# First half of a conv-attention block: the diagonal taps move around the wait for normalised tokens, and VectorE's taps are interleaved anew

## The chip, the cores and the metric

One core of a Trainium2 chip runs the whole program. The metric is the device time of one execution in microseconds (us); the value of a kernel is the median of its runs. The engines are TensorE (PE in the profile; PEld is its weight load), VectorE (DVE), ScalarE (ACT), GpSimd (POOL) and the DMA queues, most of them issued by SyncE (SP).

## What is computed

The input is an image of 192 channels by 128 x 128 positions. The first half is a channel attention with a 3 x 3 depthwise convolution, the second a mixture of experts over all positions:

```python
xn  = layernorm over channels (x)                       # per position, twice nested
qkv = einsum('bchw,oc->bohw', xn, w_qkv)                # 192 -> 576 channels
qkv = depthwise 3x3 convolution (qkv, w_dw)             # 9 taps per channel
q, k, v = split(qkv) * spatial_interaction
attn = softmax(normalised(q) @ normalised(k)^T * temperature)   # 8 heads, 24 x 24 each
x = x + w_proj @ (attn @ v)
x = x + top-2 of 4 experts (192 -> 768 -> 192, gelu)
```

The change lies in the first half, in the part that makes q and k: normalise, project, nine taps of the depthwise convolution, multiply by `spatial_interaction`, and sum up the products of q and k.

## The kernel before

The first half runs over 32 blocks of four image rows (512 positions). Every engine has its own instruction stream, a function `step(i)` written out by hand and called for i = -2 to 34; the middle of it is a hardware loop over pairs of steps. The engines meet only in semaphores. One call of `step(i)` works on several blocks at once: i + 2 is loaded and its moments are taken, i + 1 is normalised, i is transposed and projected, n = i - 1 goes through the convolution, m = i - 2 is turned and goes into the sum of products.

In a step, block by block:

- VectorE normalises four rows into `tn` (L625, "tn" below). ScalarE completes the tile (L538, `tn_dup`), TensorE transposes it in eight pieces (L744), ScalarE copies the result rounded to `xh_a` and `x_c` (L491, L493), and VectorE writes the remainders `xl_a` and `x_c` (L596, L598, semaphore `lo_ok`).
- TensorE projects, `z(i, 0..4)` (L735), five passes each, and ScalarE evicts each to `zwin` (L468) or `zv` (L474). The PSUM banks for z are two, so z(i, ct) waits for the eviction of z(i, ct - 2).
- The nine taps of the three channel tiles (ct = 0, 1, 2) are shared out. TensorE does three, two and two of them with diagonal matrices: `dw(n, ct)` (L693), two passes per tap. VectorE adds five, six and six more: `tap(n, ct, k)` (L589), in which k = 0 reads TensorE's PSUM bank and the others read and write `acc` in SBUF. ScalarE makes the ninth (L484), GpSimd adds it (L411) and multiplies by `spatial_interaction` (L414).
- ScalarE takes squares of the result (L508), TensorE turns it four rows in sequence, `q_tr(m, t)` (L709), ScalarE copies it (L459), and `gram(m, t)` (L721) sums up the products.
- For block i + 2, TensorE transposes x (L764, L765), which needs the banks that `lo_ok` sets free, ScalarE copies it to `xtok` (L525), VectorE takes moments (bn_stats L618, aggregate L634), and GpSimd makes the inverse deviation of them in seven small operations (L428 to L435).

The engine's order in a step is what the change edits. TensorE: transposes of tn, dw 0, dw 1, q_tr 0, x transposes, q_tr 1, gram 0, z 0, q_tr 2, gram 1, z 1, q_tr 3, gram 2, dw 2, gram 3, z 2, z 3, z 4. VectorE: xl_a, x_c, taps 0.0, 0.1, 0.2, 1.0, 0.3, 1.1, 0.4, 1.2, 1.3, 1.4, 1.5, 2.0, then bn_stats and taps 2.1 to 2.4 in turn with tn before tap 2.4, the aggregates, tap 2.5 (c.k is channel tile and number of the tap). Successive taps of one tile each wait for the tap before. ScalarE and GpSimd keep their order.

In two early and four late steps ScalarE and GpSimd also split expert weights into two parts (L546, L447), whose stores the next such split waits for.

Of the kernel before, what the change touches and what calls it, by code (L numbers as in the profile page):

```python
# [19 lines left out]
ALU = mybir.AluOpType  # L20
# [25 lines left out]
PE_TAPS = [[0, 1, 2], [0, 1], [0, 1]]  # L46
DVE_TAPS = [[3, 4, 5, 6, 7], [2, 3, 4, 5, 6, 7], [2, 3, 4, 5, 6, 7]]
POOL_TAP = 8
HEAD_START = 2
CX = C + E  # L50
CY = CX + E
C3 = 3 * C + E
# [66 lines left out]
def build(nc, x, spat, ln_w, ln_b, w_qkv, w_dw, w_proj, temperature, gate_w, gate_b, w1, b1, w2, b2, out):  # L119
    top = ExitStack()  # L120
    with top:
# [45 lines left out]
        with p1:  # L167
# [401 lines left out]
            def _(dve):  # L569
                def window_ready(n):  # L570
                    if n.within(0, NB - 1):
                        dve.wait_ge(z_a, 5 * n.val + QK)
                    wait(dve, carry, n.val)
                    if n.static and n.val == NB:
                        dve.wait_ge(row_z, 1)
# [15 lines left out]
                        scalar=wdw[:, ct, DVE_TAPS[ct][k]:DVE_TAPS[ct][k] + 1], in1=before, op0=ALU.mult, op1=ALU.add).then_inc(dw_l[ct], 1)  # L591

                def step(i):
                    if i.within(0, NB - 1):
                        dve.wait_ge(hi_ok, 2 * i.val + 1)
                        nc.vector.tensor_tensor(xl_a[:, 0, :], tp[0][:, :], xh_a[:, 0, :].bitcast(FP32), ALU.subtract).then_inc(lo_ok, 1)  # L596
                        dve.wait_ge(hi_ok, 2 * i.val + 2)
                        nc.vector.tensor_tensor(x_c[CB:128, 0, :], tp[1][CB:128, :], x_c[CB:128, 0, :].bitcast(FP32), ALU.subtract)\  # L598
                            .then_inc(lo_ok, 1)
                    n = i - 1  # L600

                    if n.within(0, NB):
                        window_ready(n)
                        for k in range(HEAD_START):
                            tap(n, 0, k)
                        for k in range(n_dve[1]):
                            if k + HEAD_START < n_dve[0]:
                                tap(n, 0, k + HEAD_START)
                            tap(n, 1, k)
                    b, a = i + 2, i + 1  # L610
                    if n.within(0, NB):
                        tap(n, 2, 0)
                    if b.within(0, NB - 1):
                        dve.wait_ge(xt_a, 2 * b.val + 2)
                        wait(dve, r_ok, 2 * b.val - 2)
                    for t in range(ROWS):
                        if b.within(0, NB - 1):
                            last = nc.vector.bn_stats(stat[:, b.par, t, :], xtok[:, b.par, t, 0:C])  # L618
                            if t == ROWS - 1:
                                last.then_inc(bn_ok, 1)  # L620
                        if t == ROWS - 1 and a.within(0, NB - 1):
                            wait(dve, ac_t, 2 * a.val)
                            dve.wait_ge(r_ok, 2 * a.val + 2)
                            for u in range(ROWS):
                                last = nc.vector.tensor_scalar(tn[:, u, 0:C], xtok[:, a.par, u, 0:C], mv[:, a.par, u, 0:1],  # L625
                                                               rs_all[:, bass.ds(a.val * ROWS + u, 1)], ALU.subtract, ALU.mult)
                            last.then_inc(tn_ok, 1)
                        if n.within(0, NB):
                            tap(n, 2, t + 1)
                    if b.within(0, NB - 1):  # L630
                        dve.wait_ge(bn_ok, b.val + 1)
                        nc.vector.memset(pause[:, 0:1], 0.0)
                        for t in range(ROWS):
                            last = nc.vector.bn_aggr(mv[:, b.par, t, :], stat[:, b.par, t, :])  # L634
                        last.then_inc(stats, 1)
                    if n.within(0, NB):
                        for k in range(ROWS + 1, n_dve[2]):
                            tap(n, 2, k)

                def setup():  # L640

# [34 lines left out]
            def _(pe):  # L676
# [59 lines left out]
                    last.then_inc(z_t, 1)  # L736

                def step(i):
                    if i.within(0, NB - 1):
                        pe.wait_ge(tn_dup, i.val + 1)  # L740
                        wait(pe, xt_a, 2 * min(i.val + 2, NB) if i.static else 2 * i.val + 4)
                        for h in (0, 1):
                            for t in range(ROWS):
                                last = nc.tensor.transpose(tp[h][:, t * 128:t * 128 + 128], tn[:, t, h * 128:h * 128 + 128], ident[:, :])  # L744
                            last.then_inc(ac_t, 1)
                    n, m = i - 1, i - 2
                    has_i, has_n, has_m = i.within(0, NB - 1), n.within(0, NB), m.within(0, NB)
                    if has_n:
                        dw(n, 0)
                        dw(n, 1)  # L750
                    if has_m:
                        q_tr(m, 0)
# [14 lines left out]
                    if has_m:  # L767
                        q_tr(m, 1)
                        gram(m, 0)
                    if has_i:  # L770
                        z(i, 0)
                    if has_m:
# [4 lines left out]
                    if has_m:  # L777
                        q_tr(m, 3)
                        gram(m, 2)
                    if has_n:  # L780
                        dw(n, 2)
                    if has_m:
                        gram(m, 3)
                    if has_i:
                        z(i, 2)
# [1087 lines left out]
```

## Time and profile before

| | us |
|---|---|
| median of 3 runs | 2479.31 |
| lowest and highest | 2478.91, 2484.78 |
| the profiled execution | 2480.38 |
| its span in the profile | 2478.6 |
| TensorE busy | 2095.3 (85%) |
| VectorE busy | 1535.2 (62%) |
| ScalarE busy | 1233.2 (50%) |
| GpSimd busy | 1059.1 (43%) |
| mean granted TensorE clock | 0.934 of full |

All times in the profile count from the start of the span. The first half ends at about 725 us. A record of the profile has a start, a duration and an engine; "x4" on a line means that four records in a row are merged into one. Records of one engine can overlap by under 0.1 us, so what an instruction costs in a stream is the distance from start to start. Since the steps repeat, one whole step, here from the tn at 427.40 to the next, can be read in place of all.

### The profile page before, as it was taken

What the parts mean: (1) busy time and instruction counts of PE and PEld (TensorE: products, weight loads), DVE (VectorE), ACT (ScalarE), POOL (GpSimd) and SP (SyncE); (2) the same over time, 40 slices, a digit from 0 to 9 for tenths busy, and PEclk for the clock granted to TensorE, in tenths of its full rate; (3) what the DMA queues carried; (4) which work ended last, traced back from release to release, by engine and by line L of the source; (5) the groups of instructions that cost most, each with busy time, mean ns of one, the idle gap of its engine ahead of it and who ended that gap; (6) DMA issues with size and microseconds to landing.
All of it is one profiled execution on the core that took longest, in us unless ns stands there. A gap on an engine that the chain in (4) does not pass through costs nothing.

```text
span 2478.6 us, 37518 instructions
## 1 busy us (share of the span) xinstructions
PE 2095.3 (85%) x10924; PEld 1693.3 (68%) x10924; DVE 1535.2 (62%) x3350; ACT 1233.2 (50%) x2152; POOL 1059.1 (43%) x1154
## 2 busy tenths in 40 slices
PE   6788888888766786139999999999999999999992
PEld 3455555555543455129988889888888998898991
DVE  5688988898782334516766646675544666565652
ACT  3455555556443441014554545555555565566661
POOL 3556555665664321640065410277400036742424
PEclk9899999999887997559999999999999999999995
DMA  4242222222314566446676666669655658776753
GB/s 121 73 122 70 70 70 70 73 71 73 90 57 109 155 161 183 150 167 203 210 249 204 239 201 200 201 231 319 214 168 179 195 188 297 246 254 204 247 186 108
DMA packets 297499, 410.82 MB, mean 166 GB/s; under 512 B 27642, under 2 KB 228602, under 8 KB 297340
## 3 DMA queue, kind: packets, MB, share of 16 engines
q1 hardware_dynamic: 272764, 350.13, 44.9%
q0 software_dynamic: 24576, 58.75, 7.3%
q8 instruction: 77, 1.26, 0.2%
q14 instruction: 82, 0.67, 0.1%
HBM read 265.73 MB, written 143.07 MB: 165 GB/s over the span
## 4 chain that ended last, share of the span: by engine, by line
PE 43%; POOL 10%; issue 4%; DMA 2%; DVE 2%; ACT 0%; SPq 0%; POOLq 0%; ACTq 0%; DVEq 0%
PE bank L1749 18%; PE bank L1767 11%; POOL xs_scratch L1336 7%; PE bank L1768 5%; POOL yg L1349 4%; PE bank L1800 4%; PE bank L1792 3%; PE bank L1773 2%; DMA xs_scratch<-xn,idx 1%; DMA yg<-y_scratch,ydx 0%; PE bank L1818 0%; PE bank L1821 0%; DVE fin L1677 0%; DVE x L1448 0%; DVE hl L1719 0%
## 5 line engine op out<-in xcount | busy, mean ns | idle before, releaser
L1767 PE MATMUL bank<-w_hl,hh 128*128 x1824 | 552.7, 356 | 25.5 <-DVE hl L1719 21.9
L1719 DVE TENSOR_TENSOR hl<-hf,hh 128x512 fp32r<-128x512 f32 x456 | 314.3, 690 | 385.0 <-ACT hh L1390 384.2
L1387 ACT ACTIVATE hf<-bank,b_col 128x512 f32<-128x512 f32 x456 | 314.3, 689 | 465.7 <-PE bank L1749 465.5
L1768 PE MATMUL bank<-w_hl,hl 128*128 x1824 | 460.4, 252 | 0.0
L589 DVE SCALAR_TENSOR_TENSOR acc<-zwin,wdw,acc 128x512 f32<-128x512 f32 (+2 forms) x462 | 423.6, 935 | 6.5
L1767 PEld LDWEIGHTS bank<-w_hl,hh 128*128 128x128 f32 x1824 | 345.4, 189 | 51.6 <-issue 30.4
L1768 PEld LDWEIGHTS bank<-w_hl,hl 128*128 128x128 f32 x1824 | 350.3, 192 | 21.2
L1349 POOL DMA_INDIRECT yg<-y_scratch,ydx x256 | 257.9, 1007 | 223.2 <-DMA y_scratch<-yo 77.3
L1336 POOL DMA_INDIRECT xs_scratch<-xn,idx x256 | 258.4, 1010 | 131.5 <-issue 75.9
L1749 PE MATMUL bank<-p2xh_a,w1b 128*128 128x512 f32 x912 | 308.3, 419 | 4.2 <-DVE p2x_c L1713 2.1
L1390 ACT ACTIVATE hh<-hf 128x512 fp32r<-128x512 f32 x456 | 287.9, 631 | 14.5
L1749 PE MATMUL bank<-p2x_c,w1b 128*128 128x512 f32 x912 | 289.8, 399 | 0.0
L1356 POOL TENSOR_TENSOR rstd<-mv,pw 128x4 f32<-128x4 f32 x32 | 7.0, 220 | 602.8 <-DVE mv L1462 602.7
L411 POOL TENSOR_TENSOR last_tap<-acc,last_tap 128x512 f32<-128x512 f32 (+2 forms) x99 | 135.2, 1365 | 250.6 <-DVE acc L589 248.5
L693 PE MATMUL bank<-zwin,diag 128*128 128x512 f32 (+2 forms) x462 | 213.2, 603 | 8.5 <-issue 8.5
L1749 PEld LDWEIGHTS bank<-p2x_c,w1b 128*128 128x128 f32 x912 | 173.3, 190 | 41.2
L1749 PE MATMUL bank<-p2xl_a,w1b 128*128 128x512 f32 x456 | 182.5, 400 | 0.0
L1663 DVE TENSOR_REDUCE yo<-bank 128x192 f32<-128x384 f32 x304 | 148.3, 551 | 34.3 <-PE bank L1768 34.1
L693 PEld LDWEIGHTS bank<-zwin,diag 128*128 128x128 f32 x462 | 87.2, 203 | 89.0 <-issue 87.5
L414 POOL TENSOR_TENSOR qs<-last_tap,s_bc 128x512 f32<-128x512 f32 (+2 forms) x99 | 144.0, 1455 | 7.8
L1749 PEld LDWEIGHTS bank<-p2xh_a,w1b 128*128 128x128 f32 x912 | 140.1, 192 | 6.2 <-ACT hf L1387 3.3
L1792 PE MATMUL bank<-ident,xs 128*128 128x128 f32 x608 | 85.7, 285 | 64.1 <-DMA xs<-xs_scratch 64.1
(252 smaller groups left out, 3484.4 us busy)
## 6 DMA issues: line engine op xcount, KB each, us to landing
w1b<-w1s_scratch SPq DMA_DIRECT2D x152, 768.0 KB, 4.7
xs<-xs_scratch SPq DMA_DIRECT2D x76, 512.0 KB, 5.5
y_scratch<-yo SPq DMA_DIRECT2D x76, 384.0 KB
zr<-v_scratch SPq DMA_DIRECT2D x64, 240.0 KB, 3.3
xtok_scratch<-xtok SPq DMA_DIRECT2D x32, 384.0 KB, 2.6
v_scratch<-zv SPq DMA_DIRECT2D x64, 192.0 KB
vc_scratch<-cv SPq DMA_DIRECT2D x64, 192.0 KB, 2.5
vd<-vc_scratch SPq DMA_DIRECT2D x64, 192.0 KB
```

The source lines that it names most:

```text
L589: nc.vector.scalar_tensor_tensor(out=a, in0=zwin[n.par][:, ct, ky + lo:ky + hi, kx:kx + W], scalar=wdw[:, ct, DVE_TAPS[ct][k]:DVE_TAPS[ct] ...
L693: last = nc.tensor.matmul(db[(n.par + ct) % 2][:, lo * W:hi * W].rearrange("p (r w) -> p r w", w=W), diag[:, ct, k, :], zwin[n.par][:, ct, ...
L1336: nc.gpsimd.indirect_dma_start(xs_dram, bass.IndirectOffsetOnAxis(ap=idx[:, h, b * NT + t:b * NT + t + 1], axis=0), src, None).then_inc(st ...
L1349: nc.gpsimd.indirect_dma_start(yg[:, s % 2, h, t, :], None, y_dram[g], bass.IndirectOffsetOnAxis(ap=ydx[:, h, s * ROWS + t:s * ROWS + t + ...
L1387: nc.scalar.activation(hf[:, k % 3, :], lb[k % 2][:, :], ACT.Gelu, bias=b1_col[:, bass.ds(exp_of[J] * CH + k, 1)]).then_inc(gelu, 1)
L1390: nc.scalar.activation(hh[:, k % 3, :], hf[:, k % 3, :], ACT.Copy).then_inc(hh_ok, 1)
L1663: nc.vector.tensor_reduce(out=yo[:, J % 2, t, :], in_=yb[t][:, 0:2 * C].rearrange("p (h c) -> p c h", h=2), axis=AX, op=ALU.add).then_inc( ...
L1719: nc.vector.tensor_tensor(hl[:, k % 3, :], hf[:, k % 3, :], hh[:, k % 3, :].bitcast(FP32), ALU.subtract).then_inc(hl_ok, 1)
L1749: last = nc.tensor.matmul(lb[k % 2][:, :], w[:, q, :], v[:, J % 2, :], start=(i == 0), stop=(i == 4))
L1767: nc.tensor.matmul(yb[t][:, 0:2 * C], hh[:, k % 3, cols], w, start=(k == 0), stop=False, skip_group_check=True)
L1768: last = nc.tensor.matmul(yb[t][:, 0:C], hl[:, k % 3, cols], w[:, 0:C], start=False, stop=(k == CH - 1), skip_group_check=True)
L1792: last = nc.tensor.transpose(mb[h][:, t * 128:t * 128 + 128], xs[:, J % 2, t, h * 128:h * 128 + 128], ident[:, :])
```

## The change

TensorE: `dw(n, 0)` is issued ahead of the wait for `tn_dup` and the transposes of tn. `dw(n, 2)` moves from behind gram 2 to the place between gram 0 and z 0. VectorE: the three first taps of tile 0 (`HEAD_START` 3 in place of 2) are issued ahead of the waits for `hi_ok` and of xl_a and x_c. Then tile 1's taps alternate with the last two of tile 0 and, from tap 1.2 on, with 2.0 to 2.2. The four bn_stats stand together, followed by tap 2.3, tn, tap 2.4, the aggregates and tap 2.5. No instruction is added or removed.

```diff
--- before.py
+++ after.py
@@ -46,7 +46,7 @@
 PE_TAPS = [[0, 1, 2], [0, 1], [0, 1]]
 DVE_TAPS = [[3, 4, 5, 6, 7], [2, 3, 4, 5, 6, 7], [2, 3, 4, 5, 6, 7]]
 POOL_TAP = 8
-HEAD_START = 2
+HEAD_START = 3
 CX = C + E
 CY = CX + E
 C3 = 3 * C + E
@@ -591,51 +591,51 @@
                         scalar=wdw[:, ct, DVE_TAPS[ct][k]:DVE_TAPS[ct][k] + 1], in1=before, op0=ALU.mult, op1=ALU.add).then_inc(dw_l[ct], 1)
 
                 def step(i):
+                    n, a, b = i - 1, i + 1, i + 2
+                    has_n = n.within(0, NB)
+                    if has_n:
+                        window_ready(n)
+                        for k in range(HEAD_START):
+                            tap(n, 0, k)
                     if i.within(0, NB - 1):
                         dve.wait_ge(hi_ok, 2 * i.val + 1)
                         nc.vector.tensor_tensor(xl_a[:, 0, :], tp[0][:, :], xh_a[:, 0, :].bitcast(FP32), ALU.subtract).then_inc(lo_ok, 1)
                         dve.wait_ge(hi_ok, 2 * i.val + 2)
                         nc.vector.tensor_tensor(x_c[CB:128, 0, :], tp[1][CB:128, :], x_c[CB:128, 0, :].bitcast(FP32), ALU.subtract)\
                             .then_inc(lo_ok, 1)
-                    n = i - 1
-
-                    if n.within(0, NB):
-                        window_ready(n)
-                        for k in range(HEAD_START):
-                            tap(n, 0, k)
-                        for k in range(n_dve[1]):
-                            if k + HEAD_START < n_dve[0]:
-                                tap(n, 0, k + HEAD_START)
+                    if has_n:
+                        for k in range(n_dve[0] - HEAD_START):
                             tap(n, 1, k)
-                    b, a = i + 2, i + 1
-                    if n.within(0, NB):
-                        tap(n, 2, 0)
+                            tap(n, 0, k + HEAD_START)
+                        for k in range(n_dve[0] - HEAD_START, n_dve[1]):
+                            tap(n, 1, k)
+                            if k + 1 < n_dve[1]:
+                                tap(n, 2, k - (n_dve[0] - HEAD_START))
                     if b.within(0, NB - 1):
                         dve.wait_ge(xt_a, 2 * b.val + 2)
                         wait(dve, r_ok, 2 * b.val - 2)
-                    for t in range(ROWS):
-                        if b.within(0, NB - 1):
+                        for t in range(ROWS):
                             last = nc.vector.bn_stats(stat[:, b.par, t, :], xtok[:, b.par, t, 0:C])
-                            if t == ROWS - 1:
-                                last.then_inc(bn_ok, 1)
-                        if t == ROWS - 1 and a.within(0, NB - 1):
-                            wait(dve, ac_t, 2 * a.val)
-                            dve.wait_ge(r_ok, 2 * a.val + 2)
-                            for u in range(ROWS):
-                                last = nc.vector.tensor_scalar(tn[:, u, 0:C], xtok[:, a.par, u, 0:C], mv[:, a.par, u, 0:1],
-                                                               rs_all[:, bass.ds(a.val * ROWS + u, 1)], ALU.subtract, ALU.mult)
-                            last.then_inc(tn_ok, 1)
-                        if n.within(0, NB):
-                            tap(n, 2, t + 1)
+                        last.then_inc(bn_ok, 1)
+                    if has_n:
+                        tap(n, 2, 3)
+                    if a.within(0, NB - 1):
+                        wait(dve, ac_t, 2 * a.val)
+                        dve.wait_ge(r_ok, 2 * a.val + 2)
+                        for t in range(ROWS):
+                            last = nc.vector.tensor_scalar(tn[:, t, 0:C], xtok[:, a.par, t, 0:C], mv[:, a.par, t, 0:1],
+                                                           rs_all[:, bass.ds(a.val * ROWS + t, 1)], ALU.subtract, ALU.mult)
+                        last.then_inc(tn_ok, 1)
+                    if has_n:
+                        tap(n, 2, 4)
                     if b.within(0, NB - 1):
                         dve.wait_ge(bn_ok, b.val + 1)
                         nc.vector.memset(pause[:, 0:1], 0.0)
                         for t in range(ROWS):
                             last = nc.vector.bn_aggr(mv[:, b.par, t, :], stat[:, b.par, t, :])
                         last.then_inc(stats, 1)
-                    if n.within(0, NB):
-                        for k in range(ROWS + 1, n_dve[2]):
-                            tap(n, 2, k)
+                    if has_n:
+                        tap(n, 2, 5)
 
                 def setup():
 
@@ -736,17 +736,18 @@
                     last.then_inc(z_t, 1)
 
                 def step(i):
-                    if i.within(0, NB - 1):
+                    n, m = i - 1, i - 2
+                    has_i, has_n, has_m = i.within(0, NB - 1), n.within(0, NB), m.within(0, NB)
+                    if has_n:
+                        dw(n, 0)
+                    if has_i:
                         pe.wait_ge(tn_dup, i.val + 1)
                         wait(pe, xt_a, 2 * min(i.val + 2, NB) if i.static else 2 * i.val + 4)
                         for h in (0, 1):
                             for t in range(ROWS):
                                 last = nc.tensor.transpose(tp[h][:, t * 128:t * 128 + 128], tn[:, t, h * 128:h * 128 + 128], ident[:, :])
                             last.then_inc(ac_t, 1)
-                    n, m = i - 1, i - 2
-                    has_i, has_n, has_m = i.within(0, NB - 1), n.within(0, NB), m.within(0, NB)
                     if has_n:
-                        dw(n, 0)
                         dw(n, 1)
                     if has_m:
                         q_tr(m, 0)
@@ -767,6 +768,8 @@
                     if has_m:
                         q_tr(m, 1)
                         gram(m, 0)
+                    if has_n:
+                        dw(n, 2)
                     if has_i:
                         z(i, 0)
                     if has_m:
@@ -777,9 +780,6 @@
                     if has_m:
                         q_tr(m, 3)
                         gram(m, 2)
-                    if has_n:
-                        dw(n, 2)
-                    if has_m:
                         gram(m, 3)
                     if has_i:
                         z(i, 2)
```

## Rows read from the trace of the kernel before

**Rows 1.** Busy time by stage: the steps from 137.9 to 611.4 (columns in the first line)
```profile
core 0: us, PE busy (x) PEld busy (x) DVE busy (x) ACT busy (x) POOL busy (x), PEclk, DMA share, GB/s
137.90:611.40 473.50, 413.21 (x1909) 271.42 (x1909) 424.65 (x738) 273.87 (x552) 282.54 (x299) 0.97 0.25 73
```
**Rows 2.** Timeline of VectorE, one step: start, us, engine, line, operation, count, idle before
```profile
427.40 1.23 DVE L625 TENSOR_SCALAR tn<-xtok,mv,rs_all 128x192 f32<-128x192 f32 x4
...
429.52 0.71 DVE L589 SCALAR_TENSOR_TENSOR acc<-zwin,wdw,acc 128x512 f32<-128x512 f32 x1
430.62 0.69 DVE L596 TENSOR_TENSOR xl_a<-bank,xh_a 128x512 fp32r<-128x512 f32 x1 [0.39 <-ACT xh_a L491]
...
432.92 0.75 DVE L589 SCALAR_TENSOR_TENSOR acc<-zwin,wdw,bank 128x512 f32<-128x512 f32 x1 [0.89 <-PE bank L693]
...
447.55 1.23 DVE L625 TENSOR_SCALAR tn<-xtok,mv,rs_all 128x192 f32<-128x192 f32 x4
```
**Rows 3.** Busy time by stage: the step before that one
```profile
405.90:427.40 21.50, 18.86 (x83) 12.55 (x83) 18.49 (x33) 11.99 (x24) 12.16 (x13) 0.92 0.24 67
```
**Rows 4.** Busy time by stage: two stretches around the start of that step
```profile
403.70:407.10 3.40, 1.43 (x7) 0.70 (x5) 3.40 (x9) 0.69 (x1) 0.55 (x1) 1.00 0.00 0
407.10:410.50 3.40, 2.77 (x10) 2.26 (x11) 2.48 (x10) 2.37 (x5) 1.51 (x2) 0.50 0.00 0
```
**Rows 5.** Timeline of TensorE, the step of rows 2
```profile
429.22 1.09 PE L744 MATMUL bank<-ident,tn 128*128 128x128 f32 x8 [2.64 <-ACT tn L538]
430.14 4.46 PE L693 MATMUL bank<-zwin,diag 128*128 128x512 f32 x10
...
434.76 0.27 PE L764 MATMUL bank<-ident,xc_a 128*128 128x128 f32 x1
...
437.22 0.48 PE L735 MATMUL bank<-xh_a,wq_ah 128*128 128x512 f32 x1
...
440.32 0.49 PE L709 MATMUL bank<-ident,qs 128*128 128x128 f32 x3
...
440.98 1.91 PE L693 MATMUL bank<-zwin,diag 128*128 128x512 f32 x4
...
446.34 0.40 PE L735 MATMUL bank<-x_c,wq_cl 128*100 128x512 f32 x1
```
**Rows 6.** Who waited for whom, 137.9 to 611.4: total us, times, longest
```profile
PE bank L744 <- ACT tn L538: 60.3, 23, 2.7
```
**Rows 7.** Timeline of ScalarE, the same step
```profile
428.66 0.42 ACT L538 ACTIVATE tn<-tn 128x256 f32<-128x256 f32 x1 [2.43 <-DVE tn L625]
...
441.85 0.68 ACT L468 ACTIVATE zwin<-bank,bz 128x512 f32<-128x512 f32 x1
```
**Rows 8.** Timeline of VectorE, single taps of the same step
```profile
433.70 0.75 DVE L589 SCALAR_TENSOR_TENSOR acc<-zwin,wdw,acc 128x512 f32<-128x512 f32 x1
434.49 0.75 DVE L589 SCALAR_TENSOR_TENSOR acc<-zwin,wdw,acc 128x512 f32<-128x512 f32 x1
...
436.48 0.75 DVE L589 SCALAR_TENSOR_TENSOR acc<-zwin,wdw,acc 128x512 f32<-128x512 f32 x1
437.14 0.75 DVE L589 SCALAR_TENSOR_TENSOR acc<-zwin,wdw,acc 128x512 f32<-128x512 f32 x1
...
438.59 1.66 DVE L589 SCALAR_TENSOR_TENSOR acc<-zwin,wdw,acc 128x512 f32<-128x512 f32 x1
```
**Rows 9.** Timeline of GpSimd, the same step: third pair, first pair's addition
```profile
430.38 1.29 POOL L411 TENSOR_TENSOR last_tap<-acc,last_tap 128x512 f32<-128x512 f32 x1 [4.65 <-DVE acc L589]
431.75 1.28 POOL L414 TENSOR_TENSOR qs<-last_tap,s_bc 128x512 f32<-128x512 f32 x1
...
438.06 1.63 POOL L411 TENSOR_TENSOR last_tap<-acc,last_tap 128x512 f32<-128x512 f32 x1 [0.78 <-DVE acc L589]
```
**Rows 10.** Timeline of GpSimd and VectorE, a late step: the first of four tn
```profile
632.50 1.59 POOL L414 TENSOR_TENSOR qs<-last_tap,s_bc 128x512 f32<-128x512 f32 x1
633.17 1.05 DVE L625 TENSOR_SCALAR tn<-xtok,mv,rs_all 128x192 f32<-128x192 f32 x1
```
**Rows 11.** Timeline of ScalarE, an early step with expert weights
```profile
96.42 0.52 ACT L546 ACTIVATE wph<-stage 128x384 fp32r<-128x384 f32 x1 [9.18 <-DMA w1s_scratch<-wpl]
```

## The prediction, made before the changed kernel ran

> Tap c.k below is the k-th tap that VectorE adds for channel tile c, `tap(n, c, k)`; dw0 to dw2 are TensorE's diagonal taps `dw(n, 0..2)`; "tn" is the normalising step of L625. All times are us.
>
> **What bounds the kernel now.** I first split the span by stage. The lines of the change run from about 30 to 725; the 23 steps between 137.9 and 611.4 take 473.5 us, 20.6 each, and in them VectorE is busy 90% and TensorE 87% [rows 1]. So neither is free, and the order decides. Two whole steps show the period: 20.15 at full clock (tn at 427.40 and again at 447.55 [rows 2]), and 21.5 for the one before [rows 3]. In the longer one the granted clock is at the lower of its two levels, 1.2 GHz, for 3.4 us, just after TensorE had sat idle 2.6 [rows 4, 5]. Steps of this second kind make up what 23 x 20.15 = 463.5 leaves over: 10.0 us in all. The waits name one gap per step on TensorE: 60.3 us in 23 waits for ScalarE's copy of tn, which itself waits for VectorE's tn [rows 6]. This is the wait that the change fills. The loop through it closes like this: tn 1.23, ScalarE's copy and the start of TensorE 0.59 (428.63 to 429.22), eight transposes 0.92, dw0 at 0.43 a pass for six passes 2.58, a start of 0.2, then tap 0.0 at 432.92 and 14.63 of VectorE without a real gap up to the next tn [rows 2, 5, 7]. The sum is 20.15.
>
> Those 14.63 are not all work. A tap takes 0.75, and the next starts 0.66 after it if it adds to another tile (436.48 to 437.14), 0.79 after it if it adds to the same one (433.70 to 434.49) [rows 8]. While GpSimd runs one of its two 1.28 us additions or products, a tap with both inputs in SBUF takes 1.66 instead, and ends 0.55 after GpSimd's operation; GpSimd, caught in turn behind a tap, takes 1.63 [rows 8, 9]. A tn under GpSimd took 1.05 in place of 0.37, ending 0.12 after it [rows 10]; it happened once, so it is a weak row. xl_a, with one input in PSUM, took 0.69 beside GpSimd [rows 2, 9]. So three pairs of GpSimd operations per step are three places where VectorE can lose up to 0.9 twice. Today the third pair falls on xl_a, x_c and VectorE's idle time and costs nothing.
>
> **The change part by part.** TensorE: dw0 goes ahead of the wait for tn. It is 2.58 of work against 2.64 of idle time [rows 5, 6], so alone it would take away the wait. Nothing needed by dw0 is late: its window was evicted before. What queues behind it is the eight transposes, from 1.8 to about 3.9 after the start of tn, then ScalarE's two copies of them; xl_a no longer cares, since it now stands behind tap 0.2. dw2 ahead of z(i,0) costs something: between q_tr(m,3) and z(i,2) there used to be 1.75 of dw2 that covered ScalarE. Without it z(i,2) could begin 0.94 after q_tr(m,3), but the eviction of z(i,0) ends at 442.53, 2.2 after 440.32, and TensorE starts 0.14 after such a copy (429.08 to 429.22) [rows 5, 7]: 1.4 of TensorE idle comes back there. No DMA issue is moved; the x transposes come about 1.1 later after tn, and the loads and stores that wait for them have most of a step to spare: zero, and a few tenths if that cover went.
>
> VectorE: the instructions are the same, 17 taps, 2 splits, 4 bn_stats, 4 tn, 4 aggregates. Pairs on the same tile fall from five to two, worth 3 x 0.13 = 0.4. But taps 0.0 to 0.2 now stand where the third GpSimd pair runs, and tn where the second runs. I lay the new step out from the start of tn at 0, by the durations above:
> - tap 2.5 starts at 2.1 as today (429.52), and GpSimd's third pair runs from 3.0 to 5.65 [rows 2, 9].
> - Tap 0.0 reads PSUM and isn't held. It starts when dw0 is done, at 4.1 (below). Tap 0.1 is held to 6.2, 0.2 ends at 7.0, xl_a at 7.6, x_c at 8.35.
> - Taps 1.0, 0.3, 1.1, 0.4 run freely and end at 11.1. GpSimd's first pair starts at 11.3, is caught behind tap 1.2 (12.9), and its second half ends at 14.3. Tap 2.0 reads PSUM and starts at 12.9, with dw2's end (below). Tap 1.3 ends 0.55 after GpSimd, at 14.85.
> - Taps 2.1, 1.4, 2.2, 1.5 at 0.66: the bn_stats start at 17.4 and, with as many columns as a tn, at most at its pace of 0.29 [rows 2]; tap 2.3 is due at 18.5.
> - GpSimd's second pair starts at 17.65. It holds tap 2.3 to 19.5, is held by it, and ends at 20.65. The first tn ends at 20.75 instead of a nominal 19.75, and the last at 21.6. Since that was at 1.23 in this step, the period is **20.37**.
>
> TensorE's loop within this: the x transposes start at 8.5 (x_c plus 0.15). From their start to z(i,0) it takes 2.46 today (to 437.22), dw2 adds 1.75, with 0.2 that is the 12.9. Today they reach the end of the last z pass in 11.8 (434.76 to 446.34 and 0.23 for the pass) [rows 5]; with the 1.4 above 13.2, dw0 2.58 and 0.2 make 24.5, which is 4.1 of the next step. Tap 0.0 could be 1.3 later before it passed the hold on tap 0.1, so TensorE no longer sets the step; the hand-over between VectorE and GpSimd does. TensorE is still idle for about 3 a step, in pieces of 1.7 (before the x transposes), 0.5 and 0.9.
>
> The Trainium skill's page "SBUF — State Buffer", section "Who interferes with whom", speaks against this change: whichever of a GpSimd operation and a VectorE operation with two SBUF inputs starts first has the shared ports for its whole length, the other blocks fully, and tensor_scalar can be caught as well. By the rows a held tap ends 0.55 after GpSimd [rows 8, 9], by the page it would need its whole 0.75 after it: an estimate from that page is 0.2 more for each of four holds, 0.8 a step.
>
> **Clock.** Bounds: no low stretch (0), or as many as now (10.0 in 23 steps). The longest idle piece shrinks, the total stays; I take a third, 3.3. The page "TensorE: Matmul & The Clock Gate", section "A second HAM failure mode: psum-queue depth-cycling", says that frequent short pauses make the clock swing too, by which all of the 10.0 would stay; no row here decides it.
>
> **Sum.** Steady stretch: 23 x 20.37 + 3.3 = 471.8 against 473.5, -1.7. In two steps ScalarE hangs on stores of expert weights (one wait 9.2 [rows 11]); there VectorE can do three taps ahead of xl_a (2.2), but dw2 at the lower clock then limits tap 2.0: I take 0.8 of each, bounds 0 and 2.2, so -1.6. In the last two steps, with four same-tile pairs fewer, -0.5. Together -3.8 on an execution of 2480.38 (span 2478.6), 1.07 above the median: 2479.31 - 3.8 = **2475.5**.
>
> **The rivals.**
> - *Holds are cheaper* (0.20): tn isn't held (rows 10 show it once), or GpSimd gets in at other moments. The hand-over loses up to 1.0, and TensorE's own loop is next: 3.65 from tap 0.0 to x_c with nothing held, 0.15, 13.2, 2.58, 0.2, so 19.8. With 0.14 for the clock that is 0.65 below today's 20.59: -15.0 in 23 steps, -2.1 outside them, 2462, and 2456 to 2471 for parts of it.
> - *The filled wait counts in full* (0.03): 2.64 x 31 steps, 2398. Against it stands that VectorE is 90% busy already.
> - *One more tap is held* (0.20): if GpSimd's third pair starts later than tap 0.0, because ScalarE's last tap or the small chain delays it, both 0.1 and 0.2 are held in front of x_c, 0.9 more. It decides as soon as 0.2 is held at all, as this loop has no slack. All of it makes 21.4 a step with the clock, 18.7 more in 23 steps, less the 2.1: 2496. Half makes 2486; middle 2491.
> - *It doesn't do what it says* (0.07): TensorE still waits for tn after dw0, because tn slides with it. Steps as now, 2479.
> - The forecast itself has 0.50, with its own range of 2470 to 2485.
>
> Faster or slower by 0.3% is 7.4 us, about what a measurement of this kernel tells from no change: below 2471.9 lie the first two rivals and a tail of the forecast, 0.26; above 2486.7 the third and a tail, 0.22; between 0.52. The range is 2462 to 2491: it takes in most of the cheaper holds and half of the added one.
>
> **What the profile will show.** TensorE's wait for ScalarE's tn should fall from 60.3 to near zero, with new waits on VectorE's x_c (1.7) and on ScalarE's eviction before z(i,2) (0.9). VectorE should idle about 1.2 before tap 0.0 and 1.1 before 2.0; tap 0.1, 1.3, 2.3 and the first tn should be long ones, tap 0.2 short. If all four tn take 0.37, or the period is under 20, the held tn was the wrong step; if tap 0.2 is long as well, the order of the third pair was.

## The result, and the profile after

The changed kernel takes 2497.74 us (median of 4 runs, 2494.59 to 2498.43) against 2479.57 for the kernel before: a ratio of 1.0066, 95% interval 1.0049 to 1.0084. It is slower, and above the forecast range of 2462 to 2491.

The profiled execution is the shortest of the four, 2494.59 us with a span of 2492.8, 14.2 above the span before. By stage, with the borders put at the same places of the work:

| stage | before | after | difference |
|---|---|---|---|
| up to the 6th tn | 137.9 | 134.5 | -3.4 |
| 23 steps, 6th to 29th tn | 473.5 | 488.6 | +15.1 |
| from there to the last tap | 130.1 | 128.5 | -1.6 |
| the rest, unchanged code | 1737.1 | 1741.2 | +4.1 |

The busy time of two single steps, of the 23 steps and of the rest (columns as in [rows 1]):

```profile
core 0: us, PE busy (x) PEld busy (x) DVE busy (x) ACT busy (x) POOL busy (x), PEclk, DMA share, GB/s
432.00:452.30 20.30, 18.44 (x87) 12.06 (x86) 17.39 (x33) 11.88 (x25) 12.60 (x14) 1.00 0.23 71
345.90:368.40 22.50, 20.11 (x81) 12.69 (x80) 17.42 (x33) 11.76 (x24) 12.57 (x14) 0.85 0.22 64
134.50:623.10 488.60, 441.03 (x1909) 285.62 (x1908) 398.92 (x737) 272.37 (x552) 289.35 (x300) 0.94 0.24 71
751.60:2492.80 1741.20, 1498.87 (x8234) 1302.13 (x8234) 917.37 (x2269) 834.72 (x1340) 631.38 (x689) 0.92 0.63 202
```

There are two kinds of steps here as before [rows 2, 3], but the mix is another. A step at full clock takes 20.34 (20.15 before). The others take 21.3 to 22.8, the granted clock is down in each of them (0.85 or 0.92 over the step), and they are 13 of the 23, where there were 7 before: the mean is 21.24 a step, 20.59 before. Of the +15.1, 23 x 0.19 = 4.4 is the longer full-clock step; the low clock takes 488.6 - 23 x 20.34 = 20.8 where it took 10.0 before, +10.8.

VectorE in a step at full clock, tn at the end (timeline, columns as in [rows 2]; the lines are L589 taps, L602/L604 the splits, L618 bn_stats, L626 tn):

```profile
457.15 0.75 DVE L589 SCALAR_TENSOR_TENSOR acc<-zwin,wdw,bank 128x512 f32<-128x512 f32 x1 [1.07 <-PE bank L693]
457.93 2.27 DVE L589 SCALAR_TENSOR_TENSOR acc<-zwin,wdw,acc 128x512 f32<-128x512 f32 x2
460.12 0.68 DVE L602 TENSOR_TENSOR xl_a<-bank,xh_a 128x512 fp32r<-128x512 f32 x1
460.83 0.69 DVE L604 TENSOR_TENSOR x_c<-bank,x_c 64x512 fp32r<-64x512 f32 x1
...
466.10 0.75 DVE L589 SCALAR_TENSOR_TENSOR acc<-zwin,wdw,bank 128x512 f32<-128x512 f32 x1 [1.14 <-PE bank L693]
466.76 3.90 DVE L589 SCALAR_TENSOR_TENSOR acc<-zwin,wdw,acc 128x512 f32<-128x512 f32 x5
470.58 1.12 DVE L618 BATCH_NORM_STATS2 stat<-xtok 128x6 f32<-128x192 f32 x4
471.63 1.03 DVE L589 SCALAR_TENSOR_TENSOR acc<-zwin,wdw,acc 128x512 f32<-128x512 f32 x1
472.59 2.21 DVE L626 TENSOR_SCALAR tn<-xtok,mv,rs_all 128x192 f32<-128x192 f32 x4
```

and GpSimd beside it:

```profile
456.24 1.28 POOL L411 TENSOR_TENSOR last_tap<-acc,last_tap 128x512 f32<-128x512 f32 x1 [2.75 <-DVE acc L589]
457.59 1.27 POOL L414 TENSOR_TENSOR qs<-last_tap,s_bc 128x512 f32<-128x512 f32 x1
```

Taps 0.1 and 0.2 together take 2.27 instead of 1.54: the first is held until 459.41, 0.55 after GpSimd's 458.86. The four tn take 2.21 instead of 1.23. So the holds stand where the layout put them. VectorE waits 1.07 before tap 0.0 and 1.14 before tap 2.0 (forecast 1.2 and 1.1). In seven of the ten steps at full clock the wait before tap 0.0 is longer, 1.59 to 1.66, and taps 0.1 and 0.2 take only 1.70 to 1.77: tap 0.0 starts about 0.5 later, tap 0.1 ends with GpSimd all the same, and the step keeps its 20.34. So it is the hand-over between VectorE and GpSimd that sets the full-clock step, and not TensorE's dw0, as the layout said.

Who waited for whom in the 23 steps (total, times, longest), to set beside [rows 6]:

```profile
DVE acc L589 <- PE bank L693: 86.6, 46, 4.1
PE bank L765 <- DVE x_c L604: 26.3, 22, 1.6
PE bank L735 <- ACT zwin L468: 14.0, 23, 0.6
```

The wait for tn is gone, and the two new waits that were forecast stand in its place, both shorter than forecast: up to 1.6 for x_c (1.7), 0.61 before z(i,2) (0.9). VectorE's waits for TensorE's diagonal taps were 32.1 in all and 2.6 at the longest before. A place where the clock falls, TensorE's timeline and then the two stretches around it (columns as in [rows 4]):

```profile
417.89 0.49 PE L709 MATMUL bank<-ident,qs 128*128 128x128 f32 x3
419.88 0.33 PE L765 MATMUL bank<-ident,xc_a 128*128 128x128 f32 x1 [1.50 <-DVE x_c L604]
420.14 0.27 PE L766 MATMUL bank<-ident,xc_b 64*128 64x64 f32 x1
420.34 0.33 PE L765 MATMUL bank<-ident,xc_a 128*128 128x128 f32 x1
420.60 0.27 PE L766 MATMUL bank<-ident,xc_b 64*128 64x64 f32 x1
```

```profile
417.80:421.20 3.40, 1.90 (x10) 1.06 (x8) 3.34 (x6) 3.04 (x9) 3.03 (x5) 1.00 0.61 186
421.20:424.60 3.40, 3.40 (x12) 2.42 (x12) 2.06 (x4) 1.66 (x5) 2.37 (x4) 0.51 0.39 114
```

TensorE waits 1.50 for x_c, then makes the x transposes, small products at a distance of 0.2 to 0.26, and after that its clock is at the lower level for 3.4 us, just when dw2 is due. Tap 2.0 waits for dw2, and with it VectorE: the longest such wait has grown from 2.6 to 4.1.

### The profile page after: what moved, and what is told of

The parts are those of the page before. It is cut to its first block, busy times and chain, and to the rows that moved or that the text cites. A ratio compares the mean times of both kernels' runs of the same rounds, so it can differ in the third digit from the quotient of the medians.

```text
span 2492.8 us, 37518 instructions
## 1 busy us (share of the span) xinstructions
PE 2124.7 (85%) x10924; PEld 1707.6 (69%) x10924; DVE 1503.1 (60%) x3350; ACT 1231.4 (49%) x2152; POOL 1070.4 (43%) x1154
## 3 DMA queue, kind: packets, MB, share of 16 engines
q8 instruction: 77, 1.26, 0.2%
## 4 chain that ended last, share of the span: by engine, by line
PE 43%; POOL 9%; issue 4%; DMA 2%; DVE 2%; ACT 1%; SPq 0%; POOLq 0%; ACTq 0%; DVEq 0%
PE bank L1749 18%; PE bank L1767 11%; POOL xs_scratch L1336 6%; PE bank L1768 5%; PE bank L1800 4%; POOL yg L1349 3%; PE bank L1792 3%; PE bank L1773 2%; DMA xs_scratch<-xn,idx 1%; DMA yg<-y_scratch,ydx 1%; PE bank L1818 0%; PE bank L1821 0%; DVE x L1448 0%; DVE fin L1677 0%; DVE hl L1719 0%
## 5 line engine op out<-in xcount | busy, mean ns | idle before, releaser
L589 DVE SCALAR_TENSOR_TENSOR acc<-zwin,wdw,acc 128x512 f32<-128x512 f32 (+2 forms) x462 | 363.0, 826 | 2.6
L693 PE MATMUL bank<-zwin,diag 128*128 128x512 f32 (+2 forms) x462 | 231.1, 633 | 10.7 <-issue 10.7
L589 DVE SCALAR_TENSOR_TENSOR acc<-zwin,wdw,bank 128x512 f32<-128x512 f32 (+2 forms) x99 | 72.3, 731 | 118.4 <-PE bank L693 117.4
L414 POOL TENSOR_TENSOR qs<-last_tap,s_bc 128x512 f32<-128x512 f32 (+2 forms) x99 | 136.5, 1379 | 7.8
```

The costliest lines, as they stand in the source:

```text
L414: nc.gpsimd.tensor_tensor(qs[:, n.par, ct, lo:hi, :], last_tap[:, ct, lo:hi, :], s_bc[:, n.par, lo:hi, :], ALU.mult).then_inc(qs_ok, 1)
L589: nc.vector.scalar_tensor_tensor(out=a, in0=zwin[n.par][:, ct, ky + lo:ky + hi, kx:kx + W], scalar=wdw[:, ct, DVE_TAPS[ct][k]:DVE_TAPS[ct] ...
L693: last = nc.tensor.matmul(db[(n.par + ct) % 2][:, lo * W:hi * W].rearrange("p (r w) -> p r w", w=W), diag[:, ct, k, :], zwin[n.par][:, ct, ...
```

## The experiments

The second half, whose code no kernel here changes, took from 1736 to 1965 us depending on the chip, so ratios are always to the kernel before on the same chip. What decides is the mean of the 23 steady steps from the profile. It repeats: the changed kernel has 21.24 twice, and e10 and e15, one kernel on two chips, have 19.33 both. A "low stretch" is a stretch of some us in which the granted clock is at the lower of its two levels. "Extra matmuls" multiply the identity with itself into a part of a PSUM bank that nobody reads: they keep TensorE busy and do no work of the kernel.

```python
def fill(k):
    for _ in range(k):
        nc.tensor.matmul(gb[0:G2, 256:384], ident[:, 0:G2], ident[:, :], start=False, stop=False, skip_group_check=True)
```

| kernel | mean steady step | granted clock in them | ratio to before |
|---|---|---|---|
| before | 20.59 | 0.97 | |
| changed | 21.24 | 0.94 | 1.0066 |
| changed, again | 21.24 | 0.94 | 1.0056 |
| e1 TensorE's order alone | 20.27 | 0.96 | 0.9963 |
| e2 VectorE's order alone | 28.44 | 0.82 | 1.0802 |
| e3 changed, 12 extra before the x transposes | 21.19 | 1.00 | 1.0040 |
| e5 changed, 6 extra there | 20.33 | 1.00 | 0.9982 |
| e6 changed, extra before gram 3 and z2 | 21.20 | 0.94 | 1.0047 |
| e4 before, 20 extra before tn's transposes | 21.67 | 1.00 | 1.0119 |
| e8 before, 10 extra there | 20.15 | 1.00 | 0.9960 |
| e12 before, dw0 moved | 20.41 | 0.92 | 0.9994 |
| e13 the same, 4 extra | 19.70 | 1.00 | 0.9909 |
| e9 TensorE's order, extra in three places | 19.62 | 1.00 | 0.9919 |
| e10 changed, xl_a and x_c first, extra as e6 | 19.33 | 1.00 | 0.9917 |
| e14 changed, xl_a and x_c first, no extra | 19.33 | 1.00 | 0.9888 |
| e15 as e10 | 19.33 | 1.00 | 0.9865 |

**The two engines' orders apart.** e1 takes TensorE's `step` of the changed kernel and VectorE's of the kernel before, e2 the other way round (with `HEAD_START = 3`).

> Only TensorE's order is changed (dw0 ahead of the wait for tn, dw2 ahead of z0); VectorE keeps the order of before. If the loss comes from TensorE's order, this is as slow as the changed kernel, 2495 or so. Theory that VectorE's hand-over with GpSimd sets the changed kernel's full-clock step of 20.35: without it xl_a and x_c go first again, the full-clock step falls to 19.5 to 19.9, TensorE idles in several short pieces, and the time depends on the clock: with the 0.9 per step that the low stretches cost the changed kernel, 2479 to 2483; with no low stretches 2463.

> Only VectorE's order is changed; TensorE still makes dw0 behind the transposes of tn. xl_a now stands behind three taps that wait for dw0, and these behind GpSimd's third pair, and taps 2.0 to 2.2 wait for a dw2 that comes late: laid out from the durations the step is 24.4 at full clock, 2580 to 2600 in all. If the order of VectorE were harmless by itself, about 2480.

e1: 20.27 a step, 0.9963 (0.9934 to 0.9993). So TensorE's order isn't the culprit; it gains 7 us in the steady steps. Most of its steps come in pairs of 18.1 and 22.8, with one low stretch to a pair. e9 below, the same order with the clock kept at 1.00, has 19.62, so the clock takes 0.65 a step here and not the 0.9 expected, and 0.9963 of 2479.57 is 2470, below the 2479 to 2483 expected. e2: 28.44 a step, 1.0802 (1.0750 to 1.0854), a loss of 215 us. The layout gave 24.4 at full clock and 2580 to 2600 in all, a ratio of 1.04 to 1.05; both are missed. How much of the 4.0 a step that came on top is the clock (0.82) wasn't tested. VectorE's timeline shows the two waits:

```profile
309.79 0.75 DVE L589 SCALAR_TENSOR_TENSOR acc<-zwin,wdw,bank 128x512 f32<-128x512 f32 x1 [5.19 <-PE bank L693]
...
323.31 0.75 DVE L589 SCALAR_TENSOR_TENSOR acc<-zwin,wdw,bank 128x512 f32<-128x512 f32 x1 [6.44 <-PE bank L693]
```

Tap 0.0 waits 5.2 for a dw0 that still stands behind the transposes of tn, and tap 2.0 waits 6.4 for a dw2 behind z1. VectorE's new order needs TensorE's. TensorE's doesn't need VectorE's: by itself it is faster (0.9963) than the two together (1.0066).

**Is it the clock, and which idle time?** e3 and e5 put extra matmuls into the wait before the x transposes, e6 into the wait for ScalarE:

```diff
# e3 with 12, e5 with 6
+                        if has_m and not (m.static and m.val < 1):
+                            fill(6)
                         pe.wait_ge(ld_x[b.par], 32 * b.half + 32)
# e6
                         gram(m, 2)
+                        if not (m.static and m.val < 1):
+                            fill(2)
                         gram(m, 3)
+                        if not (m.static and m.val < 1):
+                            fill(4)
                     if has_i:
                         z(i, 2)
```

> The changed kernel with 12 extra matmuls of 128 columns (1.3 us, result unused) on TensorE in each step, in the idle time before the x transposes. Theory that the low-clock stretches come from the idle time there, beside the sparse x transposes: they vanish between 134 and 623, all steps take 20.3 to 20.4, and the time falls by about 20, to 2475 to 2480. Rival, the low stretches come from the idle time before z2: no change, 2495 to 2500. Rival, the clock isn't the cause but only goes along with it: steps still of 21.3 to 22.7 at full clock.

e3 kept the clock up in every steady step, and yet each took 21.19. By itself that would fit the rival "steps still long at full clock". But one fill turned out to be two records of 0.11 us, so 12 were 2.6 us in a wait of 1.6, 1.0 too many, and pushed what follows back (0.85 a step). The time expected, 2475 to 2480, was missed (ratio 1.0040, 1.0014 to 1.0067). Half as many, e5, decides between the two:

> The changed kernel as it is, for the kernels that are compared with it on one chip. If the loss is its own and not that of one chip: 10 to 20 us above the kernel before, with undisturbed steps of 20.35 and longer ones of 21.3 to 22.8 where the granted clock is at its lower level.

> The changed kernel with 6 extra fp32 matmuls of 128 columns ahead of the x transposes. One takes 0.22 us (two records of 0.11, as the 12 of the run before showed: 2.6 us, of which 1.0 too many), so these are 1.3 us in an idle time of 1.6. Theory of the clock: no low stretch in the steady steps, all of them 20.3 to 20.4 and the time about 20 below the changed kernel's. Rival (the idle time before z2 makes the low stretches): as the changed kernel, 21.2 a step on average.

The changed kernel, measured again, repeats its loss: 1.0056 (1.0039 to 1.0073), the same 21.24 a step. With 1.3 us of extra matmuls:

```profile
136.40:604.10 467.70, 443.14 (x2188) 300.84 (x2187) 412.82 (x738) 272.45 (x552) 290.70 (x300) 1.00 0.25 75
```

```profile
387.99 1.47 PE L681 MATMUL bank<-ident 128*96 128x128 f32 x12
389.71 0.33 PE L771 MATMUL bank<-ident,xc_a 128*128 128x128 f32 x1 [0.25 <-DVE x_c L604]
```

Clock 1.00 over all 23 steps, 467.7 us for them, 20.33 each. It is 16.9 us below the changed kernel's median on that chip (2477.23 against 2494.12) and 0.9982 (0.9970 to 0.9994) of the kernel before. TensorE is given work for nothing, and the kernel is faster: the idle time itself cost nothing that shows (20.33 a step with it filled, 20.34 without), the clock that it brought down cost 20.8. The second view is TensorE's timeline in one step: of the wait for x_c, 0.25 is left.

> The changed kernel with 2 and 4 extra matmuls (0.4 and 0.9 us) before gram 3 and before z2, where TensorE waits for ScalarE; the wait before the x transposes stays empty. Theory that the low stretches come from the idle time beside the sparse x transposes: they stay, 21.1 to 21.3 a step on average. Rival (any idle time counts, whatever lies beside it): fewer of them, 20.4 to 20.8.

```profile
139.10:626.80 487.70, 460.11 (x2189) 312.23 (x2188) 399.21 (x737) 272.42 (x552) 289.49 (x300) 0.94 0.24 71
```

The other two pauses filled: no difference, 21.20 a step. The matmuls are 1.3 us as well, but only about 0.9 of it falls into idle time, since these pauses are 0.24 and 0.61. What is left idle on TensorE in a step at full clock sets the two kernels side by side: about 1.1 in e5, where the clock stays up, and 1.0 to 1.5 in e6, where it falls in 12 of 23 steps (13 in the changed kernel). Two whole steps of e6, one of each kind:

```profile
245.33:265.67 20.34, 19.36 (x99) 13.31 (x98) 17.43 (x34) 11.84 (x24) 12.66 (x14) 1.00 0.25 71
286.00:308.77 22.77, 21.24 (x93) 13.99 (x92) 17.45 (x33) 11.84 (x24) 12.62 (x14) 0.85 0.22 64
```

So not any idle time counts, but that before the x transposes.

For the kernel before, `fill(20)` (e4) and `fill(10)` (e8) stand ahead of `pe.wait_ge(tn_dup, i.val + 1)`.

> The kernel before with 20 such extra matmuls (2.1 to 2.3 us) in the 2.6 us in which TensorE waits for tn. If idle time causes its low stretches too, all its steps take 20.15 and it gains the 10.0 of the steady stretch: 2468 to 2471. If the steps of 21.5 have another cause: 2479.

> The kernel before with 10 extra matmuls, 2.2 us, in the 2.6 us of waiting for tn (20 of them took 4.4 us, held back the transposes by 1.5 and made every step 21.67 at full clock). Expected: every steady step 20.15 at full clock, 10 us below the kernel before. If idle time has no part in it: 20.6 on average, no difference.

e4: every step 21.67 at full clock. 4.4 us in a wait of 2.6 are 1.7 to 1.8 too many, and 1.5 of that went into each step. e8:

```profile
139.00:602.40 463.40, 453.18 (x2372) 316.85 (x2371) 424.47 (x737) 273.18 (x552) 285.40 (x299) 1.00 0.25 75
```

463.4 for 23 steps, 20.15 each, as expected, and 0.9960 (0.9948 to 0.9972). The long steps of the kernel before were the clock too.

**TensorE's moves one by one.** e12 is the kernel before with dw0 ahead of the wait for tn and nothing else; e13 has 4 extra matmuls before q_tr 0; e9 moves dw2 too and has 2, 2 and 4 before q_tr 0, gram 3 and z2.

```diff
# e12
...
+                    if has_n:
+                        dw(n, 0)
                     if i.within(0, NB - 1):
                         pe.wait_ge(tn_dup, i.val + 1)
...
                     if has_n:
-                        dw(n, 0)
                         dw(n, 1)
```

> The kernel before with one move only: dw0 ahead of the wait for tn. VectorE's order and dw2's place are those of before. Laid out from the durations: 19.3 a step at full clock, with TensorE idle 0.7 before the transposes and 1.3 before q_tr 0. If the clock stays up: 20.6 - 19.3 over 23 steps, 2450; with low stretches up to 1.0 a step, 2473. If dw0's move is what costs: 2490 or more.

> The same with 4 extra matmuls (0.9 us) in the idle time before q_tr 0. Clock up in every steady step, 19.3 to 19.4 each, 2448 to 2454. If 12 is already at full clock: no difference to it.

> TensorE's whole order of the change (dw0 and dw2 moved), VectorE's order of before, and fills of 2, 2 and 4 matmuls before q_tr 0, gram 3 and z2. Without fills this took steps of 18.1 and 22.8 in turn, 20.3 on average, with the clock low in the second. With the clock up 19.5 to 19.9 in both, so 0.3 to 0.5 above the kernel with dw0 alone: that difference is the price of moving dw2 away from ScalarE's eviction. If dw2's place is harmless, no difference.

e12: 20.41 a step and 0.9994 (0.9955 to 1.0032), no difference to the kernel before. The clock, at 0.92, took what the move gave: 0.7 a step against e13, which has clock 1.00, 19.70 a step, 0.9909 (0.9869 to 0.9950); I had expected 19.3. In e12 the clock falls behind another wait than in the changed kernel, but again one directly ahead of the x transposes, of 1.13 before q_tr 0 (TensorE's timeline, then the stretch behind them):

```profile
430.44 0.54 PE L709 MATMUL bank<-ident,qs 128*128 128x128 f32 x3 [1.13 <-POOL qs L414]
430.82 0.27 PE L765 MATMUL bank<-ident,xc_a 128*128 128x128 f32 x1
```

```profile
432.50:436.00 3.50, 3.50 (x13) 2.87 (x14) 3.43 (x6) 1.87 (x5) 3.04 (x5) 0.54 0.87 262
```

e9: 19.62, not 0.3 to 0.5 above e13 but level with it, so that moving dw2 away from ScalarE's eviction costs nothing that shows. That expectation fell. The idle time that comes back on TensorE is less than the 1.4 of the layout: in e1 it is 0.24 before gram 3 and 0.61 before z2. The two kernels differ in their fills too (4 and 8), so the 0.08 between them says nothing.

**The held tap in front of x_c.** e14 is the changed kernel with one block of VectorE's `step` put back; e10 and e15 are the same kernel with the fills of e6.

```diff
# e14
-                    if has_n:
-                        window_ready(n)
-                        for k in range(HEAD_START):
-                            tap(n, 0, k)
                     if i.within(0, NB - 1):
                         dve.wait_ge(hi_ok, 2 * i.val + 1)
...
                             .then_inc(lo_ok, 1)
+                    if has_n:
+                        window_ready(n)
+                        for k in range(HEAD_START):
+                            tap(n, 0, k)
```

> The changed kernel with one thing put back, xl_a and x_c ahead of taps 0.0 to 0.2, and with the small fills of 2 and 4 matmuls before gram 3 and z2, which alone changed nothing. Theory that the full-clock step of 20.34 is set by GpSimd's third pair holding tap 0.1 in front of x_c: the step falls to 19.5, bound by ScalarE's eviction before z2, 20 us less in 23 steps, 2460 to 2465 if the clock stays up. Rival (the held tn and taps 1.3, 2.3 set it, wherever xl_a stands): 20.3.

> The changed kernel with xl_a and x_c ahead of taps 0.0 to 0.2 and no extra matmuls at all. With the fills before gram 3 and z2 its steps were 19.3 at full clock. Theory that the changed kernel's loss was two things, the held tap 0.1 in front of x_c (1.0 a step) and the low clock in the wait that it made before the x transposes (0.9 a step), of which this order removes both: 19.3 to 19.8 a step, 2455 to 2465 on a chip where the kernel before takes 2480. Rival (the clock falls wherever TensorE idles for about 3 us a step, unless it is filled): 20.2 to 20.5 a step, 2473 to 2480.

> The same with the fills of 2 and 4 matmuls before gram 3 and z2, beside the plain one on one chip: 19.3 a step, 29 below the kernel before, 2451. If the fills add nothing, as they did in the changed kernel, the two are equal.

e10 has 19.33 a step (expected 19.5), and e14, with the same 19.33, shows that it owes nothing to the fills. The 23 steps of e14, and VectorE, GpSimd and TensorE in one of them:

```profile
137.00:581.30 444.30, 413.06 (x1910) 267.58 (x1909) 417.52 (x736) 272.04 (x553) 285.64 (x300) 1.00 0.26 78
```

```profile
334.98 0.69 DVE L598 TENSOR_TENSOR xl_a<-bank,xh_a 128x512 fp32r<-128x512 f32 x1 [1.27 <-ACT xh_a L491]
335.70 0.69 DVE L600 TENSOR_TENSOR x_c<-bank,x_c 64x512 fp32r<-64x512 f32 x1
336.43 0.75 DVE L589 SCALAR_TENSOR_TENSOR acc<-zwin,wdw,bank 128x512 f32<-128x512 f32 x1
337.21 1.54 DVE L589 SCALAR_TENSOR_TENSOR acc<-zwin,wdw,acc 128x512 f32<-128x512 f32 x2
...
342.64 4.81 DVE L589 SCALAR_TENSOR_TENSOR acc<-zwin,wdw,acc 128x512 f32<-128x512 f32 x5
```

```profile
333.87 1.28 POOL L411 TENSOR_TENSOR last_tap<-acc,last_tap 128x512 f32<-128x512 f32 x1 [2.74 <-DVE acc L589]
335.23 1.28 POOL L414 TENSOR_TENSOR qs<-last_tap,s_bc 128x512 f32<-128x512 f32 x1
```

```profile
336.64 0.54 PE L709 MATMUL bank<-ident,qs 128*128 128x128 f32 x3 [0.25 <-POOL qs L414]
337.02 0.27 PE L765 MATMUL bank<-ident,xc_a 128*128 128x128 f32 x1
```

GpSimd's third pair falls on xl_a and x_c again, which it doesn't hold; taps 0.1 and 0.2 take 1.54 together and come after it. x_c ends 3.39 after the start of tap 2.5 (333.00 to 336.39) and not 6.15 after it (455.37 to 461.52), TensorE no longer waits for it, and the clock stays at 1.00 with nothing filled in. Ratio 0.9888 (0.9845 to 0.9930), which is 2452 on a chip where the kernel before takes 2479.57 (2455 to 2465 expected); e15 on the same chip 0.9865 (0.9822 to 0.9909), the same within the intervals. This order beats both kernels.

Two things limit what e14 says. The rival with 3 us of idle time a step isn't tested by it, since e14 leaves TensorE idle for only 1.2 to 1.6; but e6 leaves it no more, 1.0 to 1.5, and there the clock falls. And the edit moves three taps, one hold and the two subtractions together. The hold on tap 0.1 goes (0.73), but the five taps after tap 2.0 take 4.81 where they took 3.90, so VectorE isn't held less in all. What shrinks is its own idle time, from 2.3 to 2.9 in a full-clock step of the changed kernel to 0.9 to 1.4: xl_a and x_c now run in it.

## Why the prediction was wrong

*What was right.* The layout of the step. It gave 20.37 at full clock, and the trace has 20.34. The held tap 0.1, tap 2.3 at 1.03 and the first tn at 1.35, the waits before taps 0.0 and 2.0, the two new waits of TensorE and the vanished one are all in the profile. The single tn under GpSimd [rows 10] was worth trusting: it is held in all 23 steps. Held taps with two SBUF inputs end 0.55 after GpSimd here too (tap 0.1 at 459.41 after 458.86). The Trainium skill's page "SBUF — State Buffer", section "Who interferes with whom", calls the shared ports an exclusive lock, under which the other operation blocks fully. An estimate that puts the held operation's whole duration after GpSimd's end gave 0.8 more, 21.2 at full clock, and no step at full clock takes that: the tap is held, as the page says, but not for its whole duration. Outside the steady steps I had -2.1 and -5.0 came (-3.4 and -1.6). The two steps in which ScalarE hangs on the stores of expert weights fell by 0.9 and 2.2 (32.78 to 31.86, 33.76 to 31.54), where I had 0.8 each.

*The step that failed* is the term **Clock**. I took 3.3 us in 23 steps, a third of the 10.0 of the kernel before, since the longest idle piece shrinks from 2.6 to 1.7. It shrank to about 1.5, the total didn't stay but fell from 2.6 to between 1.8 and 2.4 in a full-clock step, and yet the term was 20.8. And the upper bound was no bound: "as many as now" assumes that no idle time can be worse than the one that goes. With 20.8 in its place the sum gives 23 x 20.34 + 20.8 = 488.6 instead of 471.8, 16.8 more, and 2475.5 + 16.8, less the 2.9 that the edges gave beyond the forecast, is 2489.4. The 8.3 from there to the median are 4.1 of the unchanged rest and 4.2 of profiled executions against their medians (before's lay 1.1 above its median, this one 3.15 below). When the changed kernel was measured again the rest took 1735.9, 1.2 less than before, so I take this part for chance; no run tests it.

Length was the wrong measure. Idle time of 1.5 directly before the x transposes brings the clock down in 13 of 23 steps, 2.6 before the transposes of tn did so in 7, and 1.3 filled in before the x transposes (e5) removes every low stretch, while filling the pauses elsewhere (e6) leaves 12 steps of 23 with them and leaves about as much idle time as e5. The Trainium skill's page "TensorE: Matmul & The Clock Gate", section "A second HAM failure mode: psum-queue depth-cycling", whose sentence on frequent short pauses I had set beside the term, was nearer than my third: by it all of the 10.0 would stay. The traces agree that short pauses bring the clock down, but at 20.8 even that was too little.

*The rivals.* "One more tap is held" ended on the right side for the wrong reason: tap 0.2 is short in every step at full clock. "Holds are cheaper" was wrong. The wait for tn did go, so the rival in which TensorE still waits is out, and filling it didn't count in full. What I missed is neither: the change puts xl_a and x_c behind three taps, the second of which GpSimd's third pair holds, so x_c comes late. My text says that this pair costs nothing today, and prices the new position (tap 0.1 to 6.2, x_c to 8.35), but did not ask what follows for TensorE's clock from x_c being late.

*The loss divided.* From e14's 19.33, the changed place of xl_a and x_c makes 1.01 at full clock (20.34, and 20.33 in e5) and 0.90 of low clock (21.24). That the 1.01 is the hold on tap 0.1 alone isn't shown, as said at e14. Against the kernel before, whose 20.59 are 20.15 and 0.44 of clock, the change with xl_a and x_c left in front gains 1.26 a step, 29 us in 23 steps; as it is, it loses 0.65 a step, 15 us.

What isn't settled: why a wait ahead of the x transposes weighs more than others. The transposes alone aren't enough, since in e14 they run behind a wait of 0.25 in the step shown and 0.7 at the most, and the clock stays at 1.00; no run changes the transposes themselves. The runs show the place, not the measure that the chip applies.

## What to carry to other kernels

Where an engine waits is as important as how long: before you move work into TensorE's idle time, look where the remaining idle time will lie, and what follows it, since a fall of the clock can cost more than the wait. That sparse products behind the wait make it worse is only argued here. A few matmuls whose result nobody reads, no longer than the wait itself, are a cheap test of whether the clock is the cause; too many of them cost nearly all of their surplus (0.85 of 1.0 in e3, 1.5 of 1.7 in e4). And when VectorE and GpSimd take turns, put the operations that it didn't hold here (those with one input in PSUM: xl_a kept its 0.69 beside GpSimd) beside its work, above all if another engine waits for what comes next.

## What the runs showed of the hardware

- The granted clock fell behind one wait of 1.50 us and the x transposes after it; 1.3 us of extra matmuls in that wait kept it at 1.00 for 468 us. In e12 it fell behind a wait of 1.13 directly before q_tr 0 and the x transposes.
- The low stretches cost 10.0 us in 23 steps before and 20.8 after, and made steps of up to 22.8 out of 20.34; in e1 they made pairs of 18.1 and 22.8.
- The idle time of TensorE alone doesn't tell whether the clock falls: 1.0 to 1.5 in a full-clock step with low stretches in other steps (e6), 1.2 to 1.6 with none (e14).
- An fp32 matmul of 128 columns took 0.22 us, as two records of 0.11.
- A tn (128 x 192, both scalars per row) took 1.35 instead of 0.37 under GpSimd's product, once in every step.
- A tap of 0.75 with two SBUF inputs that GpSimd held ended 0.55 after GpSimd's operation (459.41 after 458.86).
